# Softmax of the first image pair in two parts, and image statistics made on ScalarE as sums and centred squares

## The reference

```
g   = groupnorm(x, 32 groups of 2 channels, eps 1e-5)      # mean and variance of each pair of channels
sel = softmax(conv1x1(g, coupler_w) + coupler_b, axis=1)   # 8 weights for each pixel
sel = sel / sel.sum(axis=1)
w   = weight as (8*64, 64, 3, 3)                           # 8 sets of 64 filters
y   = conv3x3(g, w, pad 1) -> (8 images, 8 sets, 64, 48, 48) + bias
out = x + sum over sets s of y[:, s] * sel[:, s]
```

## Time and profile before

| | |
|---|---|
| median of 3 runs | 349.02 us (348.99 to 349.83) |
| the profiled execution, its own time | 348.88 us |
| its span in the trace | 346.8 us |
| mean granted clock of TensorE | 0.977 |
| busy share PE, DVE, ACT, POOL | 95%, 83%, 27%, 66% |

### The profile page before, as it was taken

The page is one execution under the profiler, slowest core; times in us unless marked ns, Lnnn a source line. Parts: engine busy times, 40 slices in busy tenths (PEclk is TensorE's granted clock), DMA queues, the critical chain, the costliest instruction groups (busy, mean ns, idle before and its releaser), DMA issues.

```text
span 346.8 us, 5530 instructions
## 1 busy us (share of the span) xinstructions
PE 328.6 (95%) x1730; PEld 157.4 (45%) x1730; DVE 286.2 (83%) x503; ACT 93.8 (27%) x131; POOL 229.4 (66%) x329
## 2 busy tenths in 40 slices
PE   8959799989999999999999999999999999999993
PEld 8924234434444344444544344444544344444441
DVE  2789999888599799887699699987799687777776
ACT  1659111145521111155511111164411111111110
POOL 4420099999984667999874577999874389533343
PEclk9987699999999999999999999999999999999998
DMA  6534969704991199007990299008840397002002
GB/s 216 214 88 87 275 136 233 164 0 108 235 245 42 30 235 218 7 0 185 180 246 16 66 218 205 0 0 212 176 100 0 89 239 163 0 15 55 0 0 68
DMA packets 30226, 41.30 MB, mean 119 GB/s; under 512 B 2112, under 2 KB 23232, under 8 KB 29824
## 3 DMA queue, kind: packets, MB, share of 16 engines
q1 hardware_dynamic: 29328, 37.49, 46.1%
q10 hardware_dynamic: 880, 3.58, 3.5%
HBM read 11.97 MB, written 4.72 MB: 48 GB/s over the span
## 4 chain that ended last, share of the span: by engine, by line
PE 62%; DVE 20%; POOL 11%; issue 6%; DVEq 1%; POOLq 0%
PE pair L372 35%; PE pair L384 12%; PE pair L380 9%; PE w_bank L432 5%; DVE high L702 3%; DVE pair L701 3%; DVE pair L685 2%; POOL quarter L1001 2%; DVE pair L687 2%; POOL v_pts L975 2%; POOL x_res L994 1%; POOL v_tail L967 1%; DVE half L710 1%; POOL bias_part L989 1%; POOL mixed L1005 1%
## 5 line engine op out<-in xcount | busy, mean ns | idle before, releaser
L372 PE MATMUL pair<-w_head,op 128*128 128x512 f16 x864 | 236.4, 383 | 8.6 <-DMA op<-v_tail 4.0
L372 PEld LDWEIGHTS pair<-w_head,op 128*128 128x128 f16 x864 | 83.5, 99 | 114.0 <-DVE half L710 8.8
L384 PE MATMUL pair<-w_tail,op 128*128 128x512 f16 x288 | 110.1, 382 | 0.5 <-DVE w_tail L850 0.5
L529 ACT ACTIVATE m_sb<-pair 128x512 f32<-128x512 f32 x72 | 42.9, 596 | 224.6 <-PE pair L384 223.7
L1001 POOL TENSOR_TENSOR quarter<-half 128x256 f32<-128x256 f32 x71 | 52.7, 742 | 66.6 <-DVE half L710 66.4
L701 DVE TENSOR_TENSOR pair<-pair,sel_now 128x512 f32<-128x512 f32 x71 | 49.5, 697 | 36.4 <-PE pair L384 35.7
L710 DVE TENSOR_TENSOR half<-pair,high 128x512 f32<-128x512 f32 x71 | 49.1, 692 | 9.8 <-DVE high L702 0.5
L380 PE MATMUL pair<-w_tail,op_two 128*128 128x512 f16 x144 | 55.2, 384 | 0.0
L685 DVE TENSOR_TENSOR pair<-pair,m_sb 128x512 f32<-128x512 f32 x72 | 49.6, 689 | 0.0
L687 DVE TENSOR_TENSOR pair<-m_sb,pair 128x512 f32<-128x512 f32 x72 | 49.3, 685 | 0.0
L702 DVE TENSOR_TENSOR high<-pair,sel_now 128x512 f32<-128x512 f32 x71 | 48.3, 681 | 0.0
(11 more groups left out here) (96 smaller groups left out, 178.1 us busy)
## 6 DMA issues: line engine op xcount, KB each, us to landing
op<-v_head SPq DMA_DIRECT2D x14, 600.0 KB, 8.2
x_res<-x_pix SPq DMA_DIRECT2D x8, 576.0 KB, 6.2
op_two<-v_head SPq DMA_DIRECT2D x14, 300.0 KB, 9.2
op<-v_tail SPq DMA_DIRECT2D x14, 300.0 KB, 7.3
op<-v_head SPq DMA_DIRECT2D x14, 288.0 KB, 8.4
out<-y_out SPq DMA_DIRECT2D x7, 576.0 KB, 4.0
x_raw<-x ACTq DMA_DIRECT2D x3, 1152.0 KB, 11.0
w_raw<-weight SPq DMA_DIRECT2D x3, 768.0 KB, 8.5
```

Of the source, the lines that this page charges most:

```text
L372: nc.tensor.matmul(dst, op[b][:, 0, j, at + r * PW:at + r * PW + P], w_head[:, j, r, :], start=fresh and r == 0, stop=False, skip_group_ch ...
L384: return nc.tensor.matmul(dst, op[b][:, 1, j, at:at + P], w_tail[:, j, 0, :], start=False, stop=True, skip_group_check=True)
L529: act.activation(m1_sb[:, i % LOOK, :], pair[i % SETS_OF_BANKS][:, 0, :], ACT.Copy).then_inc(m1_copied, 1)
```

## The change

**Softmax of the first pair.** Its eleven DVE instructions and the exponential are now given a part of the pixels. Part 0 (`SOON` = 6 tiles, 12 of 36 columns of pixels, 96 of 288 elements in a partition) stands where the whole stood. Part 1 (the other 12 tiles, 192 elements) is made inside round 0, behind tiles 0 to 3, its exponential in ACT's slot of tile 3. DVE waits for it at tile 6, POOL at the parts of the bias that go past tile 5.

**Statistics.** For the pairs 1 to 3, the six `bn_stats` and the `bn_aggr` of a round leave DVE. ACT makes instead, in its slots of tiles 3, 4 and 5, two sums over half an image pair each (a copy into `v_pts` with an accumulator), a centre from the first of them (one element in each partition), and two sums of squares around the centre. DVE combines them with five instructions of one element behind tile 4 (`combine`).

**Order.** `group_sums` moves behind PE's iteration 5, the variance behind DVE's tile 6, `inverse_deviation` behind POOL's tile 6, and `scale_and_shift` behind DVE's tile 7. In round 0 alone POOL's bias parts stand behind tiles 0, 3, 4, 10 and 13 (`BIAS_FIRST_AT`). Round 0 is written out ahead of the loop on DVE and POOL.

The diff, cut to its core:

```
+SOON = 6
+SOON_PIX = 2 * SOON
+BIAS_AT = (0, 0, 1, 2, 3, 4)
+BIAS_FIRST_AT = (0, 0, 3, 4, 10, 13)
+SUMS_AT = (3, 3)
+SQUARES_AT = (4, 5)
...
@@ PE, round_
-                    if more and i == 4:
+                    if more and i == 5:
                         group_sums(n + 1)
...
@@ ACT
+            def sum_of(m, j):
+                act.wait_ge(x_ahead, m * 16)
+                act.wait_ge(t_first, 2)
+                act.wait_ge(t_done, (m - 1) * NP + 2)
+                act.activation(v_pts[:, j, :], half_of(x_raw, j), ACT.Copy, accum_out=x_sum[:, j:j + 1]) \
+                    .then_inc(x_moments, 1)
+            def center_of(m):
+                act.wait_ge(x_moments, m * 4 - 3)
+                act.activation(center[:, :], x_sum[:, 0:1], ACT.Copy, scale=2.0 / HW).then_inc(centered, 1)
+            def square_of(m, j):
+                act.wait_ge(centered, m)
+                act.wait_ge(x_moments, m * 4 - 2 + j)
+                act.activation(v_pts[:, j, :], half_of(x_raw, j), ACT.Square, bias=center[:, 0:1], scale=-1.0,
+                               accum_out=x_square[:, j:j + 1]).then_inc(x_moments, 1)
...
+                    for j in range(2):
+                        if more and i == SUMS_AT[j]:
+                            sum_of(n + 1, j)
+                            if j == 0:
+                                center_of(n + 1)
+                        if more and i == SQUARES_AT[j]:
+                            square_of(n + 1, j)
+                    if n == 0 and i == 3:
+                        exponentials(0, 1)
...
@@ DVE
+            def combine(m):
+                dve.wait_ge(x_moments, m * 4)
+                dve.tensor_scalar(mean_var[:, 0:1], x_sum[:, 0:1], x_sum[:, 1:2], 1.0 / HW, ALU.add, ALU.mult) \
+                    .then_inc(moment_steps, 1)
+                dve.tensor_scalar(mean_square[:, :], x_square[:, 0:1], x_square[:, 1:2], 1.0 / HW, ALU.add, ALU.mult) \
+                    .then_inc(moment_steps, 1)
+                dve.wait_ge(moment_steps, m * 4 - 2)
+                dve.tensor_tensor(offset[:, :], mean_var[:, 0:1], center[:, :], ALU.subtract).then_inc(moment_steps, 1)
+                dve.tensor_tensor(minus_offset[:, :], center[:, :], mean_var[:, 0:1], ALU.subtract).then_inc(moment_steps, 1)
+                dve.wait_ge(moment_steps, m * 4)
+                dve.scalar_tensor_tensor(mean_var[:, 1:2], offset[:, :], minus_offset[:, 0:1], mean_square[:, :],
+                                         ALU.mult, ALU.add).then_inc(prep, 2)
...
-                    if more and i == 1:
-                        dve.wait_ge(x_ahead, (n + 1) * 16)
-                        statistics(range(CHUNKS // 2))
-                    if more and i == 2:
-                        statistics(range(CHUNKS // 2, CHUNKS))
-                    if more and i == 3:
-                        aggregate(n + 1)
-                    if more and i == 5:
+                    if begin and i == 0:
+                        with_bias(0, 1)
+                        maximum(0, 1)
+                    if begin and i == 1:
+                        less_maximum(0, 1)
+                    if begin and i == 2:
+                        add_up(0, 1)
+                        invert(0, 1)
+                        divide(0, 1)
+                    if begin and i == 3:
+                        add_up_again(0, 1)
+                        invert_again(0, 1)
+                        divide_again(0, 1)
+                        selection(0, sel_now_parts, sel_rest, 1)
+                    if more and i == 4:
+                        combine(n + 1)
+                    if more and i == 6:
                         group_variance(n + 1)
-                    if more and i == 6:
+                    if more and i == 7:
                         scale_and_shift(n + 1)
...
@@ POOL
+                if 2 * (b * TPI + (j + 1) * BIAS_TILES) > SOON_PIX:
+                    pool.wait_ge(sel_rest, 1)
...
-                    if more and i == 5:
+                    if more and i == 6:
                         inverse_deviation(n + 1)
-                    if i + 1 < 2 * BIAS_PARTS:
-                        input_and_bias((i + 1) // BIAS_PARTS, (i + 1) % BIAS_PARTS, n)
+                    for part in range(1, 2 * BIAS_PARTS):
+                        if i == (BIAS_FIRST_AT if begin else BIAS_AT)[part]:
+                            input_and_bias(part // BIAS_PARTS, part % BIAS_PARTS, n)
```

More of the change, by code:

```diff
@@ new lines, in invert_again, with divide_again, selection @@
+            def invert_again(m, part=None):
+                signal, base, px = chain(m, part)
+                dve.wait_ge(signal, base + 13)
+                dve.reciprocal(top[:, px], top[:, px]).then_inc(signal, 1)
+            def divide_again(m, part=None):
+                signal, base, px = chain(m, part)
+                dve.wait_ge(signal, base + 14)
+                dve.tensor_tensor(mix[:, px, :], logit[:, px, :], spread(top[:, px], SETS), ALU.mult).then_inc(signal, 1)
+            def selection(m, dst, done, part=None):
+                signal, base, px = chain(m, part)
+                dve.wait_ge(signal, base + 15)
+                dve.tensor_reduce(dst[1][:, px], mix[:, px, :], axis=AX.X, op=ALU.add).then_inc(signal, 1)
+                dve.tensor_scalar(dst[0][:, px, :], mix[:, px, :], undo[:, 0:1], None, ALU.mult).then_inc(done, 1)
@@ L929, in _ @@
             input_tails_of(3, 0, 4)
[L930 to L932 removed]
+            with_bias(0, 0)
+            maximum(0, 0)
+            less_maximum(0, 0)
             last_point_tails(2, 0)
```

124 lines of the change are left out of this document (75 added, 49 removed).

## The result

The changed kernel takes 346.22 us (median of 4, 345.87 to 346.84) against 349.00 (348.90 to 349.83) for the kernel before. The ratio is 0.9922, with a 95% interval of 0.991 to 0.9934: 2.8 us faster. The profiled execution took 345.96 us, its span is 344.2; before they were 348.88 and 346.8.

A forecast was written before the change was run, and what follows sets the result against it. PE was taken as the bound from 45 us on, so only its gaps could be won: 1.3 + 1.24 + 0.64 - 0.1 - 0.2 - 0.2 = 2.7 us from 348.88 gives 346.2, median 346.3; range 344.9 to 347.8.

The forecast's parts named there:

- PE's tile 7 (against 61.8): Round 0: PE starts tile 7 at 60.5, where the kernel before compares at 61.8; 1.3 us gained.
- rstd; gaps around the shift: Round 0, scale and shift one tile later: rstd at 71.0, PE's gaps at 73.18 and 75.79 gone, 0.80 + 0.44 gained.
- The start: DVE's queue ahead of tile 0's product: smaller instructions bring the product 2.0 us earlier, to 41.2; PE goes on at 43.4 to 43.6.
- Tiles 0 to 4 on DVE: Round 0: DVE bounds for a while, the second part adds 3.4 us, tile 4's half comes at 59.6 before any lock.
- The lock: Second softmax part: three DVE instructions with two SBUF inputs exclude POOL's, 0.3 each, 0.9 us; bounds 0 and 3.0.
- the rival in which it costs nothing: The lock costs nearly nothing, DVE wins the races and combine takes 0.6: 345.1 us, chance 0.2.
- the prediction's own sign: Second part: less maximum, divide and divide again would take longer than their 0.3 to 0.4 if the prediction is right.
- the prediction's sum without the lock: Round 0: without lock time tile 4's half comes at 59.6 and PE could start tile 7's points at 59.7.
- ACT, and statistics off DVE: ACT's added passes fit its slots and cost nothing; statistics leaving DVE win nothing, the 0.77 gaps at round ends stay.
- The end of round 0: Bias part behind tile 13 falls on tile 14's softmax and lengthens the gap at 117.57: 0.2 lost (0 to 0.5).
- the second rival: DVE becomes the bound in round 0, lock 2.5 and combine 2.3: 348.9 us, no change, chance 0.1.
- The slower rival: ACT's copy in slot 9 is late every round behind a late shift: 1.8 us slower at 3.5 late, 350.8, chance 0.05.

The follow-up runs named there:

- second trace: Profile of the unchanged changed kernel, run again beside the second group: median 346.06 us, ratio 0.9904 to the kernel before.
- the others of the table: Changed kernel plus: last bias part behind tile 14, 345.45 us; that and next softmax a tile sooner, 345.75; weighting on ACT, 345.05; weighting on ACT and part 14, 345.23.
- the first trace: Profile of the changed kernel taken with the main result: median 346.22 us, profiled execution 345.96 us.
- the fastest kernel: Changed kernel with the last bias part behind tile 14 and the softmax weighting on ACT in every round: 344.36 us, ratio 0.986.
- the order alone: Changed kernel with the first softmax whole ahead of tile 0 and statistics on DVE again, only the new order kept: 348.63 us, ratio 0.9983.

## Why the prediction was right, by its steps

The forecast was 346.3 and the time is 346.22. The mechanisms were mostly the ones foreseen, but that the sum came out to 0.1 us is luck: 0.5 more was won up to the logits and 0.2 more in rounds 1 and 2, and 0.7 more was lost at the end of round 0.

| step | foreseen | measured |
|---|---|---|
| product of tile 0; PE goes on | 41.2; 43.4 to 43.6 | 41.05; 43.22 |
| PE's tile 7 (against 61.8) | 60.5 | 60.16, second trace 60.46 |
| `combine`; loss behind it | 1.3; 0.1 | 1.35; 0.09 |
| rstd; gaps around the shift | 71.0; gone | 70.87; gone |
| gap ahead of the logits | 0.2 | 0.14 |
| won up to the logits | 2.9 | 3.36 |
| lost at the end of round 0 | 0.2 (0 to 0.5) | 0.89 |
| rounds 1 and 2 | 0 | 0.1 won in each |
| from first to last instruction | | 2.6 |
| time of the profiled execution | 2.7 | 2.92 |

**The start.** Right to 0.15 us for the product and 0.2 to 0.4 us for PE, and for the reason given: DVE's queue ahead of the product. Kernels with the whole softmax there go on at 45.20 and 45.19.

**Tiles 0 to 4 on DVE.** Right that DVE is the bound and that the split's 2 us shrink there, to 1.3 as foreseen and to 1.6 and 1.3 in the two traces: a first part of 9 tiles loses 0.5 at the start and 0.1 at tile 7, and the wait foreseen for half of tile 4 "near 60" stands at 60.16, though it is 0.44 and not 0.8.

**The lock.** The term was 0.9, spread as 0.3 over three instructions. The traces showed 0.50 and 0.82 in the changed kernel and from 0 to 0.86 in the others of the table, so the size was near and the rival in which it costs nothing did not come in the changed kernel; but the prices stand otherwise. An instruction is held for nothing or to near the end of the POOL instruction that it meets (0.09 to 0.71), decided by 0.1 to 0.3 us of POOL's phase. In the first trace the prediction's own sign failed: "less maximum", divide and divide again took 0.35, 0.36 and 0.36, no longer than undisturbed, and the weighting, which the prediction held to be free, was hit for 0.50, as in one other trace. That its removal brings PE's tile 7 to 59.7, the prediction's sum without the lock, bears the rest of that sum out.

**ACT, and statistics off DVE.** ACT's four passes cost nothing, and steady rounds gained 0.1 where nothing was put. That the ends of rounds keep their gap of 0.77 was right, and right in its reason: neither moving the softmax nor taking the statistics away touched it much, taking work out of tiles 12 to 17 did (0.29 from 0.27).

**The end of round 0: the mis-sized term.** "The bias part behind tile 13 falls on the softmax of tile 14, and what DVE loses there goes straight into the gap": the mechanism is the one found, but it was put at 0.2 with 0.5 as its bound, and it took 0.63 (divide 1.10 instead of 0.46). The bound was set without the nearest row, the 996 ns of one bias instruction. Another 0.26 came with "less maximum" (1.12), held by `input_tails`. POOL has reached other instructions at that moment than before, when it took 0.61. The prediction had no such term: it asked what the moved instruction meets, and not what all that follows on POOL meets.

**Slips in the working.** The low clock of the earlier trace rows is in slices 3 to 5, not 3 to 6. Four tiles of 4.10 are 16.4, not 16.2; in the kernel with the weighting on ACT PE takes 16.41 from tile 3 (43.26) to tile 7 (59.67). Half the way to the second rival is 347.6, not 347.8. None of them changes a step.

**The slower rival.** Its place (slot 9 on ACT) never made anyone wait; in round 0 the copy there starts at 75.44, some 1.2 us behind its pitch, ahead of DVE's seed at 76.12. Yet a slower outcome was near: with POOL's bias parts where they were, DVE waits 3.31 for rstd and the kernel is 0.5% slower than before. The prediction named the cause of that gap but gave the reordering no rival of its own.

What stays open: by its trace the statistics' move brings nothing without the split (with the whole softmax ahead of the product, kernels with and without it show no gap from 50 us to the logits), but their medians, 347.01 and 348.63, differ by the clock's fall, and no run here separates the two fully. Neither the split nor the statistics' move was run without the new order, and of the order only the bias parts were put back by themselves: what the later scale and shift are worth alone is not shown.

## What to carry to other kernels

A piece taken off the start of a chain is worth its length only where the engine that made it has slack right behind: here 2.1 us at the start were worth 0.8 in the end, and that only with other work gone from the stretch behind it (with the statistics there the time was 1.8 more) and the third engine's queue put in order (4.7 more without). When a queue is reordered, look at each place where its instructions now meet another engine's with two SBUF inputs, not only at the moved one, and price each such meeting from nothing up to a whole instruction. Where a gap returns every round, compare the slack of the tiles ahead of it with the work in them: moving work inside that stretch gave 0.13 us a round, 0.27 us out of it gave 0.29 back.

## What the runs showed of the hardware that was not expected

- A `tensor_scalar` of 192 fp32 elements in a partition with one SBUF tensor took 0.81 us beside a POOL instruction of 0.72 that had begun 0.03 before it, and 0.31 otherwise. With one element (L670, L694) it took 0.15 to 0.20, beside POOL or not. POOL can lose as well: its second bias instruction took 1.13 in the changed kernel and 1.21 with the weighting on ACT (begun at 51.24, the same moment as the divide) instead of 1.00; begun 0.24 behind the divide, in the fastest kernel, it took 1.00.
- An ACT pass of 1152 elements with an accumulator takes 1.16, as one without; the square with a bias tensor takes 1.25, and reading the accumulator 0.19 more.
- In the three kernels with the whole softmax ahead of the product PE is idle from 34 to 36 us (a wait of 2.10 to 2.40), and each of them saw the granted clock fall to 1.2 GHz later: at 37 us in the kernel before and in the one with the statistics on ACT, where PE had only short work between waits and it cost nothing; at 46.5, behind the wait of 2.31, in the order alone, where it cost 1.6 us. In the changed kernel PE is busy for 0.59 us between 34 and 36 us, and neither it nor any other with the split shows a fall between 34 and 46 us. The same wait of 2.31 was followed by no fall in the kernel with the statistics on ACT, nor the waits of 1.46 and 1.66 in the changed one; a wait of 2.65 with the bias parts as before was. What decides between them stays open.
